# Two more Winograd fours in the last pair of row blocks, a ring of eleven load buffers for twelve, one cover unit in two halves, and the last layer's products grouped by the sources that are ready

## The reference

```python
h = maximum(layernorm(x), 0)
x = x + layer_l(h, adj)        # layers 0 to 3, each with a product adj @ h
```

## Time and profile before

| | |
|---|---|
| median of 3 runs | 1913.24 us (1912.98 to 1913.88) |
| the profiled execution | 1913.93 us |
| its span | 1912.0 us, granted TensorE clock 0.999 |
| TensorE matmul busy | 1866.2 us, 98%, 7784 records |
| VectorE busy | 1065.0 us, 56% |
| ScalarE, GpSimd busy | 112.0 us, 9.6 us |
| HBM read | 672.27 MB, 353 GB/s over the span |

### The profile page before, as it was taken

How to read it: one execution, slowest core, us unless ns; L and a number is a source line. 1 busy time by engine, 2 the same in 40 slices (tenths; PEclk the granted TensorE clock), 3 DMA queues, 4 the chain that set the end, 5 groups by cost and what they waited for, 6 DMA issues and landing times.

```text
span 1912.0 us, 19280 instructions
## 1 busy us (share of the span) xinstructions
PE 1866.2 (98%) x7784; PEld 691.6 (36%) x7784; DVE 1065.0 (56%) x1156; ACT 112.0 (6%) x288; POOL 9.6 (1%) x26
## 2 busy tenths in 40 slices
PE   5899999999999999999999999999999999999998
PEld 1233333333333333333333333444444444344343
DVE  8988899999877763768876825322111110110322
ACT  0000000000000001100000001111000000000000
POOL 0000000000000000100000000000000000000000
PEclk9999999999999999999999999999999999999999
DMA  9999999999988886488777886597999889999998
GB/s 382 421 421 421 420 421 421 421 421 419 360 321 318 307 292 214 174 354 368 298 322 313 330 346 242 241 396 292 402 374 374 328 312 421 376 366 403 358 422 339
DMA packets 95895, 675.63 MB, mean 353 GB/s; under 512 B 11201, under 2 KB 13249, under 8 KB 14273
## 3 DMA queue, kind: packets, MB, share of 16 engines
q1 hardware_dynamic: 92880, 672.18, 87.5%
q10 hardware_dynamic: 2928, 2.23, 0.4%
HBM read 672.27 MB, written 2.10 MB: 353 GB/s over the span
## 4 chain that ended last, share of the span: by engine, by line
PE 89%; DMA 8%; DVE 2%; SPq 1%; issue 0%; ACT 0%; DVEq 0%
PE acc L667 43%; PE acc L697 23%; DMA ring<-stream_in 8%; PE Z L721 3%; PE HT L667 2%; PE acc L932 2%; PE DEG L944 2%; PE acc L853 2%; PE acc L829 2%; PE acc L843 2%; PE acc L866 1%; PE acc L884 1%; PE acc L899 1%; PE acc L891 1%; PE DEG L916 1%; PE HT L764 1%
## 5 line engine op out<-in xcount | busy, mean ns | idle before, releaser
L667 PE MATMUL acc<-ring,states 128*64 128x512 f32 x3992 | 894.4, 595 | 35.3 <-DMA ring<-stream_in 28.9
L667 PEld LDWEIGHTS acc<-ring,states 128*64 128x64 f32 x3992 | 281.3, 137 | 588.3 <-issue 554.5
L1381 DVE TENSOR_TENSOR row_sum<-row_sum,ring 128x2048 f32<-128x2048 f32 x194 | 444.6, 2292 | 18.7 <-DMA ring<-stream_in 13.8
L697 PE MATMUL acc<-ring,states 128*128 128x512 f32 x1032 | 451.4, 594 | 0.0
L697 PEld LDWEIGHTS acc<-ring,states 128*128 128x128 f32 x1032 | 193.0, 190 | 244.0 <-issue 244.0
L1218 DVE TENSOR_TENSOR z_sb<-Z,deg_rsqrt 128x256 f32<-128x256 f32 x16 | 6.8, 425 | 335.9 <-PE Z L721 335.8
L667 PE MATMUL acc<-diag,states 128*64 128x512 f32 x432 | 103.6, 595 | 0.5 <-DMA diag<-stream_in 0.5
L1442 DVE TENSOR_TENSOR y<-acc,y 64x512 f32<-64x512 f32 x36 | 24.6, 683 | 111.1 <-PE acc L667 110.8
L721 PEld LDWEIGHTS Z<-below,y 128*128 128x128 f32 x512 | 62.5, 191 | 52.0 <-issue 18.8
L721 PE MATMUL Z<-below,y 128*128 128x64 f32 x512 | 70.0, 280 | 2.2 <-DVE y L1443 2.2
L1408 DVE TENSOR_TENSOR diag<-diag,ident 128x384 f32<-128x384 f32 x12 | 6.7, 558 | 107.8 <-ACT row_sum L534 107.7
(11 more groups left out here) (157 smaller groups left out, 1294.6 us busy)
## 6 DMA issues: line engine op xcount, KB each, us to landing
ring<-stream_in SPq DMA_DIRECT2D x609, 1024.0 KB, 10.5
diag<-stream_in SPq DMA_DIRECT2D x28, 1024.0 KB, 11.7
x<-x_in SPq DMA_DIRECT2D x4, 512.0 KB, 6.9
y<-u_in SPq DMA_DIRECT2D x4, 512.0 KB, 8.6
x_out<-x ACTq DMA_DIRECT2D x16, 128.0 KB, 7.0
below<-w_in ACTq DMA_DIRECT2D x6, 16.0 KB, 5.8
bias<-b_in ACTq DMA_DIRECT2D x1, 32.0 KB, 9.6
```

The costliest lines, as they stand in the source:

```text
L667: return nc.tensor.matmul(half_of(bank, half), h[layer % 2][:, J], moving, start=start, stop=stop)
L697: done = nc.tensor.matmul(acc[bank][:, :], states[:, J * 2 * F:(J + 1) * 2 * F], source_tile(slot(key), k), start=first and k == 0, stop=l ...
L1381: nc.vector.tensor_tensor(row_sum[:, :], before, slot(key)[:, :], ALU.add).then_inc(unit_summed, 1 if count > 1 else 2)
```

## The change

The ring has 11 buffers, and the freed megabyte holds `formed_last`, the state sums of source pairs (7, 6) and (5, 4). The last pair takes six fours (19 in all, for 17) and one plain source, 3. In pairs 3 and 4 the plain sources come behind all fours. Cover unit 14 leaves the covers: its layer-2 half goes beside near_diagonal(0), its layer-1 half, loaded again, beside `behind_last`. VectorE's step for the earlier pair's lower row comes behind the forms of four 3 in all pairs, and the forms of fours 4 and 5 behind it. Groups of the last layer take every source whose states are ready, so that the group of rows behind 14 has 17 units and the final part 35, for 11 and 54.

```diff
-RING = 12
+RING = 11
...
-SOURCE_PAIRS = [(15, 14), (13, 12), (11, 10), (9, 8)]
-FOURS = [[sp for sp in SOURCE_PAIRS if sp[1] > hi] for hi, lo in PAIRS]
+SOURCE_PAIRS = [(15, 14), (13, 12), (11, 10), (9, 8), (7, 6), (5, 4)]
+FOURS = [SOURCE_PAIRS[:2], SOURCE_PAIRS[:3], SOURCE_PAIRS[:4], SOURCE_PAIRS[:4], SOURCE_PAIRS[:6]]
...
 PAIR_STEPS = [
-    [("cover", 15), ("cover", 14), ("four", 0), ("near", 0), ("four", 1), ("plain", 11)],
-    [("cover", 13), ("four", 0), ("four", 1), ("near", 1), ("four", 2), ("cover", 12), ("plain", 9)],
-    [("cover", 11), ("four", 0), ("four", 1), ("near", 2), ("four", 2), ("four", 3), ("cover", 10), ("plain", 7)],
-    [("cover", 9), ("cover", 8), ("four", 0), ("four", 1), ("near", 3), ("four", 2), ("plain", 7), ("plain", 6),
-     ("four", 3), ("plain", 5)],
-    [("cover", 7), ("four", 0), ("four", 1), ("near", 4), ("four", 2), ("plain", 7), ("plain", 6), ("four", 3),
-     ("plain", 5), ("plain", 4), ("plain", 3)],
+    [("cover", 15), ("cover", 13), ("four", 0), ("near", 0), ("four", 1), ("plain", 11)],
+    [("cover", 12), ("four", 0), ("four", 1), ("near", 1), ("four", 2), ("cover", 11), ("plain", 9)],
+    [("cover", 10), ("four", 0), ("four", 1), ("near", 2), ("four", 2), ("four", 3), ("cover", 9), ("plain", 7)],
+    [("cover", 8), ("four", 0), ("four", 1), ("near", 3), ("four", 2), ("four", 3), ("plain", 7), ("plain", 6),
+     ("plain", 5)],
+    [("cover", 7), ("four", 0), ("four", 1), ("near", 4), ("four", 2), ("four", 3), ("four", 4), ("four", 5),
+     ("plain", 3)],
 ]
...
+CUT = 14
...
-        return ([("again", *PAIRS[p - 1][::-1])] if p else []) + [(2, lo, hi)]
+        return [("again", *PAIRS[p - 1][::-1]) if p else (2, 0, CUT), (2, lo, hi)]
...
-for quad in range(3):
+for quad in range(2):
...
+GROUPS_AFTER |= {12: [(2, 0), (2, 1)], 13: [(2, 2), (2, 3)], 14: [(2, r) for r in (4, 5, 6, 7)],
+                 15: [(2, r) for r in (8, 9, 10)]}
+FINAL_ROWS = [0, 1, 14, 13, 12, 2, 3, 11, 4, 5, 8, 6, 9, 7, 10]
...
+TAKEN_UP_TO = {qr: b for b in range(HEAD, ROWS) for qr in GROUPS_AFTER[b]} | {(3, r): ROWS for r in FINAL_ROWS}
...
 def group_sources(quad, r):
-    return [g for g in range(4 * quad, 4 * quad + 4) if g > r]
+    before = [TAKEN_UP_TO[q, r] for q in range(quad) if (q, r) in TAKEN_UP_TO]
+    return list(range(max(before, default=r + 1), TAKEN_UP_TO[quad, r]))
...
-    out += [(2, 0, g) for g in COVER_AT_END[:-1]] + [("again", *PAIRS[-1][::-1]), (2, 0, COVER_AT_END[-1])]
+    out += [(2, 0, g) for g in COVER_AT_END[:-1]] + [("again", *PAIRS[-1][::-1]), ("again", 0, CUT),
+                                                  (2, 0, COVER_AT_END[-1])]
...
+        formed_last = sbuf("formed_last", [P, UNIT])
...
-            return diag[n // 2][:, at:at + FEATS].rearrange("p (k f) -> p k f", f=F)
+            return (diag + [formed_last])[n // 2][:, at:at + FEATS].rearrange("p (k f) -> p k f", f=F)
...
+                else:
+                    await_unit((2, 0, CUT), 2)
...
+                    else:
+                        behind = nc.tensor.matmul(half_of(BANK_UP[0], 0), h[0][:, CUT * TPR + k],
+                                                  source_tile(slot((2, 0, CUT)), k), start=False, stop=False)
...
-                if p > 0:
-                    behind.then_inc(unit_freed, 1)
+                behind.then_inc(unit_freed, 1)
                 near.then_inc(unit_freed, 1)
...
+                await_unit(("again", 0, CUT), 1)
...
+                    cut = nc.tensor.matmul(half_of(BANK_UP[0], 1), h[1][:, CUT * TPR + k],
+                                           source_tile(slot(("again", 0, CUT)), k), start=False, stop=False)
                 done.then_inc(unit_freed, 1)
+                cut.then_inc(unit_freed, 1)
...
-                        four_even(p, n, after_first=lambda: near_diagonal(p))
-                        if p == len(PAIRS) - 1:
+                        four_even(p, n, after_first=(lambda: near_diagonal(p)) if n == 2 else None)
+                        if p == len(PAIRS) - 1 and n == 2:
                             turn_own(1, 0)
...
-                if ("plain", 7) in PAIR_STEPS[p][:-1]:
-                    end_layer_1(before_lo)
-                if len(FOURS[p]) == 4:
+                if len(FOURS[p]) >= 4:
                     first_form(p, 3)
                     third_form(p, 3)
+                    if len(FOURS[p]) > 4:
+                        first_form(p, 4)
                     last_forms(p, 3)
-                if ("plain", 7) not in PAIR_STEPS[p][:-1]:
-                    end_layer_1(before_lo)
+                end_layer_1(before_lo)
+                if len(FOURS[p]) > 4:
+                    third_form(p, 4)
+                    last_forms(p, 4)
+                    first_form(p, 5)
+                    third_form(p, 5)
+                    last_forms(p, 5)
```

More of the change, by code:

```diff
@@ L109 @@
         pending = pending[share:]
-FINAL_ROWS = [0, 1, 14, 13, 12] + list(range(2, 12))
+GROUPS_AFTER |= {12: [(2, 0), (2, 1)], 13: [(2, 2), (2, 3)], 14: [(2, r) for r in (4, 5, 6, 7)],
+                 15: [(2, r) for r in (8, 9, 10)]}
+FINAL_ROWS = [0, 1, 14, 13, 12, 2, 3, 11, 4, 5, 8, 6, 9, 7, 10]
 GROUPS = [qr for b in range(HEAD, ROWS) for qr in GROUPS_AFTER[b]] + [(3, r) for r in FINAL_ROWS]
+TAKEN_UP_TO = {qr: b for b in range(HEAD, ROWS) for qr in GROUPS_AFTER[b]} | {(3, r): ROWS for r in FINAL_ROWS}
 def group_sources(quad, r):
-    return [g for g in range(4 * quad, 4 * quad + 4) if g > r]
+    before = [TAKEN_UP_TO[q, r] for q in range(quad) if (q, r) in TAKEN_UP_TO]
+    return list(range(max(before, default=r + 1), TAKEN_UP_TO[quad, r]))
 ORDER = (list(range(ROWS)), list(range(LAST, -1, -1)), list(range(ROWS)),
-         [0, 1, 15, 14, 13, 12] + list(range(2, 12)))
+         FINAL_ROWS[:2] + [LAST] + FINAL_ROWS[2:])
 def rank(layer, b):
```

## The result

The changed kernel took 1916.9 us (median of 20 runs, 1913.9 to 1919.8) against 1913.4 for the kernel before (20 runs, 1911.6 to 1915.9): ratio 1.0017, with a 95% interval of 1.0010 to 1.0023. So it is slower by 3.5 us, just under the 3.8 that the prediction counted as a difference, and outside its range of 1903.5 to 1914.5, which leaned to the other side. The profiled execution has a span of 1914.7 us (before: 1912.0).

A forecast was written before the change was run, and what follows sets the result against it. The prediction took TensorE's work and few idle stretches as the bound, with loads setting the pace at the end. Its terms summed to -2.4 us, putting the median at 1910.8 us, range 1903.5 to 1914.5.

The forecast's parts named there:

- first stage, ring: First quarter: with eleven buffers for twelve, loads lose nothing because DMA is saturated from full queues; 0 us.
- cover 14 in two halves: Pairs: one cover unit goes, its halves riding free beside two lone half steps; -3.4 us.
- two more fours: Last pair: sources 7 to 4 take 4 + 3 steps instead of 8 plain ones; -3.4 us.
- plain units last: Pairs 3 and 4: TensorE's waits of 1.82 and 1.09 us for four 3's first unit go; -2.9 us.
- ring, pairs 1 to 4: Four 2's second unit waits for a later release, so TensorE idles 2.1 to 2.3 us per pair; +8.7 us.
- pair 0: Four 1's first upper-row unit lands two places later, after step 4 of four 0 wants it; +0.9 us.
- groups, rows 4 to 15: Seven of layer 4's units move ahead of the end of row 15's diagonal; +12.1 us there.
- the end: From row 15 on, loads set the pace with fewer units left: 131.2 us become 116.8, -14.4 us.
- that the ring costs nothing: Rival: the load pairs 1 to 4 need is there in time, giving 1902.1 us; 13 in 100.
- Row 3's state step: Rival: VectorE's wait on ScalarE falls between forms in the last pair and stalls TensorE, 1918.9 us; 7 in 100.
- the long groups: Rival: row 14's group of 17 starts without a full ring and waits for loads, 1922.8 us; 4 in 100.
- The rides: Rival: weight loads show in the two steps carrying cover 14's halves, giving 1913.0 us; 2 in 100.

The follow-up runs named there:

- e4: The changed kernel with VectorE folding the group of a one-unit row before it scales the row ahead of it: 1914.7 us, ratio 1.0003.
- e11: The changed kernel with a22 loaded ahead of a21, ring of twelve, four fours in the last pair, and one-unit rows folded before the previous row's scaling: 1901.2 us.
- e13: The changed kernel measured again as it is, beside a run with five small unused products ahead of the waits: 1916.6 us, ratio 1.0014.

## Why the prediction was wrong

The terms against the profile's span, from the stages and gaps above:

| term | forecast | measured |
|---|---|---|
| first stage, ring | 0 | +1.3 |
| cover 14 in two halves | -3.4 | -3.4 |
| two more fours | -3.4 | -3.3 |
| plain units last | -2.9 | -2.9 |
| ring, pairs 1 to 4 | +8.7 | +9.3 |
| clock behind these waits | 0 | +1.5 |
| pair 0 | +0.9 | +0.7 |
| groups, rows 4 to 15 | +12.1 | +12.6 |
| the end | -14.4 | -13.1 |
| sum | -2.4 | +2.7 (span: +2.8) |

(The waits are entered with their idle time. With the 0.15 us that each costs besides, the four of the ring make +9.9 and the two that went -3.2; the sum hardly moves.)

The step that failed is the one on the ring of eleven, which was put at 8.7 us for four waits and nothing else. For the four waits its mechanism was right, place by place and to 0.6 us; the rest of its cost was ruled out in two sentences. "In the first quarter DMA is saturated from full queues" took a mean over 48 us for a queue: up to 41 us it is filled by loads that were issued up to 30 us earlier, and the next one waits for VectorE's first sum. That is 1.3 us. And "the 2.2 us goes straight to TensorE" priced only the idle time, not the clock behind it: 1.5 us in the profiled execution, about 1.8 on average. With 0.6 for the waits themselves, 0.5 for rows 4 to 15, 1.3 for the end and 0.1 for the fours, less 0.2 in pair 0, that is 5.1 of the 5.2 us by which the span was missed; 3.4 of them are the ring's. Between the medians the miss is 6.1 us; the other 0.9 lies outside the stages: the changed kernel's profiled execution exceeds its span by 0.6 us more than that of the kernel before, and it lies 0.4 us above its median, where the other lies 0.7 above.

The end was half right. The last load landed 106.8 us after row 15, as forecast (106.9). But TensorE was no longer waiting for it: with gaps of 0.6 us ahead of the products of rows 14, 8 and 9 it had fallen behind the loads (it ended its last unit and the product behind it 110.4 us after row 15, where 108.8 were reckoned for TensorE alone), and 11.3 us followed the last landing, not 9.9. That the landing came out to 0.1 us and the end to 1.3 is therefore in part luck. Two sums of the prediction are a tenth off (7 x 1.72 is 12.0, and the terms for TensorE alone give 108.9), which changes nothing. The prediction had seen that the two nearly tie and put up to 2 us into its range; e4 and e11 show that with eleven buffers either side alone gives little, and with twelve VectorE's order gives 3.5 us. An end that isn't paced by loads was named as a sign against the forecast, and it came.

The rivals: that the ring costs nothing fell with the four waits. Row 3's state step stalled nobody: the last pair has no gap. Rows 4 to 15 ran without idle time, so the long groups don't outrun the ring. The rides were free. None of the rivals held what happened, a cost of the ring beyond the one place that the walk had found.

What stays open: why a wait of 2.2 to 2.4 us lowers the clock one time and not the next. The slow steps don't stand out by the length of their wait (2.19 to 2.45 us, the others 2.18 to 2.36), and pair 1 was hit four times in five, pair 3 never. How the dip at 41 to 44 us becomes 1.2 us at the end of the first stage was not followed: in two of the nine profiles (e4, e13) the landings just behind the dip were not late, and the time went later. And it isn't shown why executions exceed their spans by 0.4 to 0.8 us more in some kernels than in others.

## What to carry to other kernels

A buffer taken from a ring is paid in every place where the ring's distance was just enough: walk the whole order of loads with the new distance, the start and the end included, and look at what releases each buffer, not at the mean bandwidth. Before giving up on it, turn the order within a group of loads, so that what is wanted first waits for what is freed first; here two lines gave 11 us. And price a wait of TensorE with its length and, at times, a stretch at half the clock behind it.

## What the runs showed of the hardware

The granted clock of TensorE fell to half behind idle times of 2.19 to 2.45 us in seven of twenty cases, and behind 3.75 and 4.44 in both; behind 1.82 and 1.09 it did not. The step behind then took 5.0 to 6.3 us for 3.5. With TensorE busy in the same stretch, on products that nobody reads, it stayed at 1.00 in seven of seven; in an eighth case, with a wait of 2.45 left behind the products, it stayed too, as in thirteen of the twenty. The last product of the kernel shows it as well: this is its window in the changed kernel, where it follows 2.49 us of idle time,

```profile
1909.50:1911.50 2.00, 1.94 (x8) 1.76 (x8) 0.01 (x1) 0.00 (x0) 0.00 (x0) 0.53 0.00 0
```

and in the eight profiles with that wait it took 1.96 to 1.98 us three times and 1.12 to 1.54 five times; in the three where VectorE folds first and the wait is 1.4 us shorter, 1.09 to 1.14. The Trainium skill (TensorE: Matmul & The Clock Gate, Why this matters for your kernels) advises to leave no long idle gaps between bursts of matmuls, since the clock drops; the traces agree, and show it behind gaps of little over 2 us too, in some executions and not in others.
